# Two cross-attentions turn both heads of a pair together; key pieces keep one bank; batch loops written out

## What is computed

```python
q = query @ W_Query + B_Query          # layer 2 has no biases
k = key @ W_Key + B_Key                # key = value = the context, 375 rows
v = value @ W_Value + B_Value
...
scores = jnp.einsum('bqhd,bkhd->bhqk', q, k) / D ** 0.5
probs = jax.nn.softmax(scores, axis=-1)
out = jnp.einsum('bhqk,bkhd->bqhd', probs, v)
out = out.reshape(B, Lq, H * D)
return out @ W_Output + B_Output
```

## Time and profile before

| | us |
|---|---|
| runs of the kernel | 3817.61, 3820.91, 3829.95 (median 3820.91) |
| the profiled execution, own time | 3808.83 |
| its span in the profile | 3807.0 |
| layer 0 attention: first scores of batch 0 to first scores of batch 15 | 74.6 to 459.7 |
| layer 2 attention: the same | 1752.8 to 2402.8 |
| layer 3 attention: the same | 2759.3 to 3426.1 |
| PE busy | 3181.0 (84% of the span) |
| DVE, ACT, POOL busy | 1563.8, 1538.9, 1223.3 |

### The profile page before, as it was taken

How to read it: one execution, slowest core, us unless ns; L and a number is a source line. 1 busy time by engine, 2 the same in 40 slices (tenths; PEclk the granted TensorE clock), 3 DMA queues, 4 the chain that set the end, 5 groups by cost and what they waited for, 6 DMA issues and landing times. The chain is left out here.

```text
span 3807.0 us, 67515 instructions
## 1 busy us (share of the span) xinstructions
PE 3181.0 (84%) x22302; PEld 2618.4 (69%) x22302; DVE 1563.8 (41%) x3515; ACT 1538.9 (40%) x4385; POOL 1223.3 (32%) x1334
## 2 busy tenths in 40 slices
PE   2899927993978837948999999759599999996998
PEld 2777727883856625636888888648478888885998
DVE  2777730002456530024444444310244444444776
ACT  1555513441345522214555555324255555552222
POOL 0000030003000030034676676510166666664121
PEclk8999958997989958978999999779799999996999
DMA  6555418982100014330000000058400000000001
GB/s 181 129 130 138 104 37 291 321 307 73 44 13 0 0 35 144 115 93 17 9 12 8 8 8 5 3 204 311 132 10 8 8 8 12 8 1 14 26 26 33
DMA packets 155225, 287.93 MB, mean 76 GB/s; under 512 B 53214, under 2 KB 126876, under 8 KB 137244
## 3 DMA queue, kind: packets, MB, share of 16 engines
q1 hardware_dynamic: 147420, 267.93, 23.1%
q0 software_dynamic: 7680, 18.36, 1.8%
HBM read 240.88 MB, written 45.35 MB: 75 GB/s over the span
## 5 line engine op out<-in xcount | busy, mean ns | idle before, releaser
L712 POOL TENSOR_SCALAR L_probs<-L_probs,L_inverse 112x375 f32<-112x375 f32 x512 | 645.7, 1261 | 87.1 <-issue 87.1
L826 DVE TENSOR_REDUCE L_negmax<-bank 112x1 f32<-112x375 f32 x768 | 394.7, 542 | 427.2 <-PE bank L481 361.4
L676 ACT ACTIVATE L_probs<-bank,L_negmax 112x375 f32<-112x375 f32 x768 | 434.5, 571 | 204.9 <-DVE L_negmax L826 199.7
L508 PE MATMUL bank<-ident,L_probs 112*125 112x112 f32 x2304 | 400.6, 283 | 17.6 <-POOL L_probs L712 11.3
L508 PEld LDWEIGHTS bank<-ident,L_probs 112*125 112x125 f32 x2304 | 336.3, 188 | 93.0 <-issue 62.0
L710 POOL TENSOR_TENSOR L_inverse<-L_sums,neg_one 112x1 f32<-112x1 f32 x512 | 308.1, 602 | 256.4 <-ACT L_probs L676 256.4
L656 ACT ACTIVATE L_probsT<-bank 125x336 f32<-125x336 f32 x512 | 231.6, 452 | 263.0 <-PE bank L508 263.0
L638 ACT ACTIVATE v<-bank 125x512 f32<-125x512 f32 x192 | 114.7, 598 | 266.1 <-PE bank L431 266.1
L523 PE MATMUL bank<-L_probsT,v 125*64 125x112 f32 x3072 | 206.1, 270 | 1.1 <-ACT L_probsT L656 1.1
L523 PEld LDWEIGHTS bank<-L_probsT,v 125*64 125x64 f32 x3072 | 150.8, 137 | 30.7 <-DVE L_oT L842 2.0
L1484 ACT ACTIVATE L0t_hidden<-bank,L0t_b 128x128 f32<-128x128 f32 x280 | 102.8, 367 | 165.3 <-PE bank L1444 146.1
(11 more groups left out here) (291 smaller groups left out, 6995.8 us busy)
## 6 DMA issues: line engine op xcount, KB each, us to landing
L0t_w<-in_F_w SPq DMA_DIRECT2D x70, 1024.0 KB, 5.3
L2t_w<-in_F_w SPq DMA_DIRECT2D x42, 1024.0 KB, 5.2
L_keys<-spread_k SPq DMA_DIRECT2D x64, 376.0 KB, 6.4
L_ctxT<-in_ctxT SPq DMA_DIRECT2D x48, 375.0 KB, 3.3
L1t_w<-in_F_w SPq DMA_DIRECT2D x16, 1024.0 KB, 6.1
slots_in<-zeros SPq DMA_DIRECT2D x4, 1792.0 KB, 16.5
L_q<-spread_q SPq DMA_DIRECT2D x128, 56.0 KB, 2.2
spread_k<-L_k_hi SPq DMA_DIRECT2D x16, 376.0 KB, 2.5
```

What stands on the lines that cost most here:

```text
L508: ins = pe.transpose(psT[h % len(psT)][0:SJ, j * T:(j + 1) * T], probs[h % NB][:, j * SJ:(j + 1) * SJ], core.ident[0:T, 0:T])
L676: act.activation(probs[e % NB][:, :], psS[e % 2][0:T, 0:S], ACT.Exp, bias=negmax[b.par][:, e:e + 1], accum_out=sums[b.par][:, e:e + 1]).th ...
L712: pool.tensor_scalar(probs[h % NB][:, :], probs[h % NB][:, :], inverse[b.par][:, h:h + 1], None, ALU.mult)\
L826: dve.tensor_reduce(negmax[b.par][:, h:h + 1], psS[h % 2][0:T, 0:S], AX, ALU.max, negate=True).then_inc(maxed.sem, 1)
```

## The change

In the wide attentions:

- `turn` of both heads of a pair is done together, straight after the scores of a later pair: at an even h PE turns heads h-4 and h-3, one after the other, and ACT copies both before it does the exponentials of h and h+1. The odd h has no turn any more; `lag` is 4.
- psT gets two banks (2 and 3), psO is bank 4, and the ring of the pieces has three: 5 and 6 in turn for L, Q, V, Y, and bank 7 alone for all key pieces. So K(m) waits until K(m-1) has been taken, where before it waited for K(m-2).
- the pieces stand elsewhere: key pieces at h = 0, 2, 3, 5, 7, 9, 12, 14 (before 0, 0, 1, 2, 3, 9, 14, 15), and in `first` they alternate with the value pieces.
- DVE takes the second half of the outputs at h = 3 (before 4) and the first half at h = 11 (before 12).

In all three attentions the loops over batches, on all engines, are written out: the same instructions, without a branch and without registers in the addresses and waits.

```diff
-        order = {0: ["K0", "K1"], 1: ["K2"], 2: ["K3"], 3: ["L0", "L1", "K4"], 4: ["V0"], 5: ["V1"], 6: ["Y0"],
-                 7: ["V2"], 8: ["Y1"], 9: ["K5"], 10: ["Q0"], 11: ["V3"], 12: ["Q1"], 13: ["V4"],
-                 14: ["K6"], 15: ["V5", "K7"]}
+        order = {0: ["K0"], 1: ["V0"], 2: ["K1"], 3: ["L0", "L1", "K2"], 4: ["V1"], 5: ["K3"], 6: ["Y0"],
+                 7: ["V2", "K4"], 8: ["Y1"], 9: ["K5"], 10: ["Q0"], 11: ["V3"], 12: ["K6", "Q1"], 13: ["V4"],
+                 14: ["K7"], 15: ["V5"]}
...
-    first_pieces = ["L0", "L1", "Q0", "Q1", "K0", "K1", "K2", "K3", "K4", "K5", "K6", "K7",
-                    "V0", "V1", "V2", "V3", "V4", "V5"]
+    first_pieces = ["L0", "L1", "Q0", "Q1", "K0", "V0", "K1", "V1", "K2", "V2", "K3", "V3", "K4", "V4",
+                    "K5", "V5", "K6", "K7"]
...
-    lag = 3 if wide else 2
+    lag = 4 if wide else 2
...
-            psS, psT, psO, ring = core.bank[0:2], core.bank[2:3], core.bank[3:4], core.bank[4:8]
+            psS, psT, psO, ring = core.bank[0:2], core.bank[2:4], core.bank[4:5], core.bank[5:8]
...
-                        out[p] = (2 + m % 2, ("K%d" % ((m - 2) % EC), d if m >= 2 else d - 1))
+                        out[p] = (2, ("K%d" % ((m - 1) % EC), d if m else d - 1))
...
-            with engine.Fori(0, (B - 4) // 2) as i:
-                heads(Batch(i, 1), False, False)
-                heads(Batch(i, 2), False, False)
-            heads(Batch(0, B - 3), False, False)
+            for n in range(1, B - 2):
+                heads(Batch(0, n), False, False)
...
-                        pe.wait_ge(probsT_ready.sem, probsT_ready.at(H * b.n + h))
+                        pe.wait_ge(probsT_ready.sem, probsT_ready.at(H * b.n + h - 1))
...
-                        if not (b_first and h < lag):
+                        if wide and h % 2 == 0 and not (b_first and h < lag):
+                            turn(*before(b, h, lag))
+                            turn(*before(b, h + 1, lag))
+                        if not wide and not (b_first and h < lag):
                             turn(*before(b, h, lag))
...
-                        if wide and not (b_first and h < lag):
+                        if wide and h % 2 == 0 and not (b_first and h < lag):
                             take_probsT(*before(b, h, lag))
+                            take_probsT(*before(b, h + 1, lag))
...
-                        if h == (4 if wide else 6) and not b_first:
+                        if h == (3 if wide else 6) and not b_first:
                             divide(b + -1, NG - 1)
...
-                        if NG == 2 and h == 12:
+                        if NG == 2 and h == 11:
                             divide(b, 0)
```

More of the change, by code:

```diff
@@ L291, in first_slots @@
                 if own_bank(p):
-                    out[p] = (2 + m % 2, ("K%d" % (m - 2), 0) if m >= 2 else None)
+                    out[p] = (2, ("K%d" % (m - 1), 0) if m else None)
                     continue
@@ L352, in _ @@
                     next_ctx(Batch(0, 1))
-                    with sp.Fori(0, (B - 2) // 2) as i:
-                        next_ctx(Batch(i, 2))
-                        next_ctx(Batch(i, 3))
+                    for n in range(2, B):
+                        next_ctx(Batch(0, n))
                     return
@@ L386, in _ @@
                 load(Batch(0, 1))
-                with sp.Fori(0, (B - 2) // 2) as i:
-                    spread(Batch(i, 0))
-                    next_load(Batch(i, 2))
-                    spread(Batch(i, 1))
-                    next_load(Batch(i, 3))
-                spread(Batch(0, B - 2))
-                spread(Batch(0, B - 1))
+                for n in range(B):
+                    spread(Batch(0, n))
+                    if n + 2 < B:
+                        next_load(Batch(0, n + 2))
                 sp.wait_ge(core.zeroed_sem, 16 * (core.slots_in.shape[0] // (B * T)))
@@ L578, in tail @@
                     if wide:
-                        turn(b, H - 3)
-                        turn(b, H - 2)
-                        pair_values(b, H - 4)
-                        turn(b, H - 1)
-                        pair_values(b, H - 2)
+                        for h in (H - 4, H - 2):
+                            turn(b, h)
+                            turn(b, h + 1)
+                            pair_values(b, h)
                     else:
@@ L727, in _ @@
                 pool.drain()
-                rstd(Batch(0, 0))
-                with pool.Fori(0, B - 1) as i:
-                    pool.wait_ge(var_ready.sem, var_ready.at(i + 2))
-                    pool.tensor_tensor(stats[:, 9:10], stats[:, 8:9], core.neg_half[0:T, :], ALU.pow)\
-                        .then_inc(rstd_ready.sem, 1)
+                for n in range(B):
+                    rstd(Batch(0, n))
             @block.vector
```

## The result

The changed kernel took 3856.2 us (median of 6 runs, 3845.2 to 3860.9), the kernel before, in the same comparison, 3817.7 (6 runs, 3812.5 to 3830.0). The ratio is 1.0093, with a 95% interval of 1.0071 to 1.0115: 27 to 44 us longer. The forecast was 3843, against a kernel before of 3820.9: +22 us where the runs show some +38. The sign held, and so did the wide range of 3818 to 3862; the forecast's own range, 3830 to 3856, is met only at its upper edge, so the size was low. The profiled execution of after took 3858.3 us, with a span of 3856.4.

A forecast was written before the change was run, and what follows sets the result against it. It took the distances between starts of TensorE's groups as the bound; 10.9 + 12.9 - 5 - 2 + 6 - 1 = +22 us on 3820.9 gave 3843 us (+0.6%), own range 3830 to 3856, wide range 3818 to 3862.

The forecast's parts named there:

- What bounds it: Wide attentions: TensorE is covered throughout, so a batch takes the sum of distances between starts of its groups; 43.5 and 44.7 us.
- The key wait: Wide attentions, K2 at h = 3: waits for DVE's low part of K1, 0.76 us a batch (layer 2), 0.92 (layer 3).
- the layout: Predicted timeline from the scores of h = 2 at time 0: second turn at 1.11, K2 at 4.22 to 4.25 instead of 3.48.
- The switch that moves: Pair with K or V piece: whole-array-to-halves loss moves from turn-to-values to piece-to-values; -0.41 + 0.33 + 0.08 = 0.
- rival 2: Wide attentions: the switch is free behind a piece, values' loads hide there; 3825 us, 10%, a third of it faster (3801).
- Layer 3's output piece: Values come straight behind its bias matmul, so one switch goes: 0.18 us twice a batch, -5 us (-3 to -5).
- Earlier `divide`: Wide attentions: DVE frees psO and fills `oT` one head sooner, shortening TensorE's wait for `oT`; -2 us.
- Edges: Both edges of both wide stages: shorter key waits in `first`, batch 0's saved turn moved to the end; -1 us (-4 to +4).
- Layer 0 written out: Layer 0's attention: the queries' reload from DRAM comes late in some batches, 0.45 us a batch; +6 us (0 to 18).
- rival 3: Written-out code costs in all attentions: layer 0's reload waits 1.4 us in each of 13 batches; 3855 us, 15%.
- So zero there: Wide attentions: writing the loops out costs nothing, since batch 12 in a loop and 13 written out take 43.51 and 43.52 us.

The follow-up runs named there:

- the first spaced order: Changed kernel with no two key pieces in one pair, a value piece taking K2's place behind L0 and L1: 3839.1 us; with loops put back 3830.3.

## Why the prediction was right, and where it was low

- **What bounds it** held: in every run of the wide stages the batch was the sum of distances between TensorE's groups, and each new wait in it showed in full.
- **The key wait** (0.76 and 0.92 us a batch) was right in place, cause and size: L0 to K2 went from 0.18 to 0.91 in layer 2, and spacing the pieces took it away, 0.76 and 0.89 a batch. In the layout the second turn should start at 1.02 (0.69 + 0.33), not at 1.11; nothing was worked out from the 1.11 but its end, which is 1.50 then and still ahead of the copy's need.
- **The switch that moves** (sum 0 for a pair) was right: eight pairs of layer 2 cost 0.06 together once no wait is left, with whatever `divide` gained in it. So rival 2 did not come: piece to values is 1.21, not 1.12. The Trainium skill (TensorE: Matmul & The Clock Gate, "Step-by-step: what each phase is for") says that loads are pulled ahead where row groups don't conflict or the load goes to the background buffer. The trace shows no such gain at this place.
- **Layer 3's output piece** (-0.36 a batch) came out near that: 44.7 to 44.38 without waits. The bias piece is 0.40 ahead of the values as it was ahead of the turn, timeline of after:

```profile
2906.42 0.47 PE L456 MATMUL bank<-L_bo,ones 1*112 1x128 f32 x2
2906.82 0.80 PE L517 MATMUL bank<-L_probsT,v 125*64 125x112 f32 x12
```

- **Earlier `divide`**: the wait is gone, its 0.08 a batch too small to see.
- **Edges** (-1): the wide attentions grew by 11.8 and 7.7 us, their batches from first to last by 11.1 and 7.6, so what lies outside is +0.8. The key waits in `first` did not shrink as forecast: by the weight loads they went from 1.8 to 2.9 us in layer 2 and from 2.0 to 3.9 in layer 3.
- **Layer 0 written out** (+6, 0 to 18): +7.4 in the stage, 5 by the sorting of all profiles. The mechanism, a reload that is just in time and then late in some batches, was the one named; it struck in five batches for about 0.8 us, between "none" and rival 3's "all". The 0.45 a batch was a pick between 0 and 1.4, so that it came this close is luck.
- **The step that failed** is a term that the sum didn't have. "So zero there", of the written-out wide attentions, was argued from their batches and is true of those; the stage behind them was not asked. Layer 2's experts take 3.5 us longer, or 2.4 without the two at a low clock. Three pairs of kernels that differ in loops alone put the whole price of written-out loops at 14 us (the changed kernel), 15 (the kernel before) and 8 (the first spaced order), of which 5 and 3.5 are placed. By the two pairs that differ in the wide loops alone, some 10 us go with those, within intervals that overlap.
- **What stays open.** Where the rest of that price lies; no profile locates it within the spread of the untouched stages. Of the +15 us that those stages show between the two profiles of each kernel, some is not the change's. Layer 1's +3.0 is inside what its self-attention varies by with the granted clock. Layer 0's experts were 418 in both profiles of the kernel before and 422 to 430 in all twelve others, among them kernels with the very same layer 0. I take 38 us for 22 as about 5 from the attentions, 2 to 4 from layer 2's experts, and the rest unsettled. Which of instruction transfers, addresses, the granted clock or chance it is was not tried.

## What to carry to other kernels

On an engine that is covered without a gap, count the distance from each piece to the next user of its bank before a bank is given away: with one bank the keys' ring had no slack where two key pieces stood 2.1 us apart, and the order that mended this put a value piece right behind L0 and L1, where the other ring had none. Work that shares an array layout belongs together, so a reordering is worth its number of switches (two fewer a pair gained 1.47 us of 43.57; merging the turns alone moved a switch and gained nothing). A loop written out isn't free because its body is equally long: look at just-in-time transfers beside it and at the stage behind it, and, the other way round, look at a loop's back edge.

## What the runs showed that I had not expected

- A loop's back edge can hold TensorE for 3.1 us and then leave it at a granted clock of 0.51 for 6.9 us: 6.7 us for one branch. It came in two kernels in layer 2, and neither in layer 3, built by the same code, nor in the other kernels with loops.
- The clock can be lower without any such pause: with the keys in one bank alone, and three key waits a batch, one batch of each wide stage had a mean granted clock of 0.96 and 0.97 and took 1.3 and 1.2 us longer than the next. With the changed kernel's one wait of 0.74 a batch it was 1.00 from 1820 to 2430.
- The change between the whole array and 64-wide halves costs 0.08 to 0.10 us each time it is made, in the three orders read for it, and was saved here only by making it less often.
- Stages with identical instructions differ by 9 to 12 us of 285 and 425 between kernels and executions, 3%, where the six runs of the changed kernel differ by 0.4%. In layer 1's self-attention the difference goes with a mean granted clock between 0.91 and 0.87.
